# A gated cross-attention block on one core: filler matmuls ahead of three more waits at the start, two GpSimd subtractions cut in halves, and a new written order for every engine

## What is computed

```python
# stage 0: one wide head over the context, a gate, an RMS norm
memory_proj = einsum('bme,de->bmd', memory, W_mem)
scores = einsum('bnd,bmd->bnm', hidden_states, memory_proj) / sqrt(256)
memory_context = einsum('bnm,bmd->bnd', softmax(scores), memory_proj)
gate = sigmoid(einsum('bnf,df->bnd', concat([hidden_states, memory_context]), W_gate) + b_gate)
x = rmsnorm(hidden_states + gate * memory_context, norm_w)
# stage 1: 16 heads of 64, masked keys
q = layernorm(x, ln_q_g, ln_q_b) @ Wq * 64 ** -0.5
k, v = split(media @ Wkv)
sim = where(media_mask, q k^T, min_float)
x = x + tanh(attn_gate) * (softmax(sim) v @ Wo)
# stage 2: feed-forward of width 1024
h = gelu(layernorm(x, ln_ff_g, ln_ff_b) @ W1) @ W2
return x + tanh(ff_gate) * h
```

## Time and profile before

| | |
|---|---|
| time, median of 3 runs | 209.27 us (209.02 to 211.89) |
| time of the profiled execution | 210.25 us |
| its span (first to last instruction) | 208.4 us |
| PE busy | 202.4 us, 97% |
| DVE, ACT, POOL busy | 148.0, 130.5, 71.3 us |

### The profile page before, as it was taken

The page is one execution under the profiler, slowest core; times in us unless marked ns, Lnnn a source line. Parts: engine busy times, 40 slices in busy tenths (PEclk is TensorE's granted clock), DMA queues, the critical chain, the costliest instruction groups (busy, mean ns, idle before and its releaser), DMA issues.

```text
span 208.4 us, 4502 instructions
## 1 busy us (share of the span) xinstructions
PE 202.4 (97%) x1505; PEld 169.1 (81%) x1505; DVE 148.0 (71%) x529; ACT 130.5 (63%) x414; POOL 71.3 (34%) x71
## 2 busy tenths in 40 slices
PE   7999999999999999999999999999999999999993
PEld 3567868888689799787978988888886799988992
DVE  1779997779967698778698889997479673235310
ACT  4386757849766787665665838979996820168300
POOL 2010423853336244407140664685725006000000
PEclk9999999999999999999999999999999999999999
DMA  6995060050000000000000000015000001100001
GB/s 184 301 378 193 5 203 0 5 201 0 0 3 2 3 2 0 5 2 3 0 2 3 0 2 3 0 32 174 2 0 3 0 0 34 48 25 0 24 32 58
DMA packets 9297, 10.06 MB, mean 48 GB/s; under 512 B 1330, under 2 KB 8116, under 8 KB 9268
## 3 DMA queue, kind: packets, MB, share of 16 engines
q1 hardware_dynamic: 8468, 9.32, 13.4%
q10 hardware_dynamic: 800, 0.39, 0.6%
HBM read 8.66 MB, written 1.05 MB: 47 GB/s over the span
## 4 chain that ended last, share of the span: by engine, by line
PE 90%; DMA 4%; DVE 2%; SPq 2%; issue 0%
PE bank L513 57%; PE bank L1338 9%; PE bank L1310 8%; PE bank L1452 8%; DMA ctx_sb<-in_ctx_dram 4%; PE bank L1348 3%; PE bank L1293 2%; PE bank L1378 2%; SPq L560 2%; PE bank L1218 1%; PE bank L1231 1%; DVE wkv_lo L1069 1%; DVE x_sb L1171 0%; PE bank L1364 0%; DVE ctx_probsT_even L1014 0%
## 5 line engine op out<-in xcount | busy, mean ns | idle before, releaser
L630 POOL TENSOR_TENSOR probs<-expd,row_rcp 128x512 f32<-128x512 f32 x39 | 40.2, 1050 | 54.4 <-DVE row_rcp L1004 49.7
L760 ACT ACTIVATE expd<-expd,neg_max 128x128 f32<-128x128 f32 x128 | 49.6, 392 | 2.4 <-DVE neg_max L994 2.4
L994 DVE CUSTOM_DVE_ANT_0 expd<-bank,mask_bias 128x128 f32<-128x128 f32 x128 | 28.2, 286 | 2.2 <-PE bank L1310 2.1
L513 PE MATMUL bank<-xhT_pair,wq_pair 128*128 128x256 f32 x192 | 26.1, 289 | 0.0
L513 PE MATMUL bank<-wo_pair,oT_pair 128*128 128x256 f32 x192 | 26.0, 288 | 0.0
L513 PEld LDWEIGHTS bank<-xhT_pair,wq_pair 128*128 128x128 f32 x192 | 23.8, 191 | 2.0 <-issue 1.2
L760 ACT ACTIVATION_READ_ACCUMULATOR expd<-expd,neg_max 128x1 f32 x128 | 24.5, 191 | 0.0
L513 PEld LDWEIGHTS bank<-wo_pair,oT_pair 128*128 128x128 f32 x192 | 23.9, 190 | 0.5 <-issue 0.4
L513 PE MATMUL bank<-wq_pair,gelu_pair 128*128 128x256 f32 x192 | 23.6, 284 | 0.1
L513 PEld LDWEIGHTS bank<-wq_pair,gelu_pair 128*128 128x128 f32 x192 | 23.3, 192 | 0.5 <-DVE x_sb L1171 0.4
L1338 PE MATMUL bank<-ident,probs 128*128 128x128 f32 x160 | 21.1, 275 | 0.0
(11 more groups left out here) (163 smaller groups left out, 358.5 us busy)
## 6 DMA issues: line engine op xcount, KB each, us to landing
...
```

Of the source, the lines that this page charges most:

```text
L513: last = nc.tensor.matmul(bank_ap, lhs(a), rhs(c), start=start and n == 0, stop=stop and n == 2)
L630: nc.gpsimd.tensor_tensor(probs[:, r, :].rearrange("p (h k) -> p h k", h=hb), expd[:, r, :].rearrange("p (h k) -> p h k", h=hb), row_rcp[: ...
L760: last = nc.scalar.activation(here, here, ACT.Exp, bias=neg_max[:, r, h:h + 1], scale=-1.0, accum_out=row_sum[:, r, h:h + 1])
L994: last = nc.vector.tensor_tensor_reduce(expd[:, r, h * w:(h + 1) * w], SC[n % 2][:, h * w:(h + 1) * w], mask_bias[:, first:first + w], -1. ...
```

## The change

1. `DUMMIES` has five entries instead of two: 2, 1 and 2 identity matmuls stand ahead of `("ctxT", 0)`, `("tiles",)` and `("y", 0)`; the groups of 3 and 2 stay, the second now ahead of `("weights",)`.
2. On POOL the subtraction of `splitv` (1024 columns) becomes two of 512, and each of the two `splito` too; the semaphore rises with the second.
3. All four orders are new from the first stages to the last.

```diff
-DUMMIES = (3, 2)
+DUMMIES = (2, 1, 2, 3, 2)
 TENSOR_ORDER = (
-    ("xT", 0), ("ctxT", 0), ("y", 0), ("tiles",), ("ctxT", "hot"), ("scores", "ctx", 0, 0), ("look", "PE"),
-    ("branch", "PE"), ("dummy", 0), ("v", "hot", 0, 0), ("dummy", 1), ("v", "hot", 0, 1), ("ctxT", 1),
...
+    ("xT", 0), ("dummy", 0), ("ctxT", 0), ("dummy", 1), ("tiles",), ("dummy", 2), ("y", 0), ("look", "PE"),
+    ("branch", "PE"), ("ctxT", "hot"), ("scores", "ctx", 0, 0), ("dummy", 3), ("v", "hot", 0, 0), ("dummy", 4),
...
 POOL_ORDER = (
-    ("branch", "POOL"), ("norm", "ctx", 0, 0), ("splitv",), ("rms", 0), ("norm", "ctx", 1, 0), ("splito", 0),
+    ("norm", "ctx", 0, 0), ("branch", "POOL"), ("splitv",), ("rms", 0), ("norm", "ctx", 1, 0), ("splito", 0),
...
                         gp.wait_ge(pe["v"], 2)
-                        nc.gpsimd.tensor_tensor(wkv_lo[:, INNER:2 * INNER], wkv_sb[:, INNER:2 * INNER],
-                                                value_hi[:, :].bitcast(F32), ALU.subtract).then_inc(pool["kvlo"], 1)
+                        for half in (slice(0, BANK), slice(BANK, INNER)):
+                            of_kv = slice(INNER + half.start, INNER + half.stop)
+                            last = nc.gpsimd.tensor_tensor(wkv_lo[:, of_kv], wkv_sb[:, of_kv],
+                                                           value_hi[:, half].bitcast(F32), ALU.subtract)
+                        last.then_inc(pool["kvlo"], 1)
                     elif st[0] == "splito":
                         gp.wait_ge(act["wsplit"], path.split_no(st))
-                        nc.gpsimd.tensor_tensor(wo_pair[:, LO, cols_of(st)], stage[:, cols_of(st)],
-                                                wo_pair[:, HI, cols_of(st)].bitcast(F32), ALU.subtract
-                                                ).then_inc(pool["wsplit"], 1)
+                        for at in (st[1] * 1024, st[1] * 1024 + BANK):
+                            last = nc.gpsimd.tensor_tensor(wo_pair[:, LO, at:at + BANK], stage[:, at:at + BANK],
+                                                           wo_pair[:, HI, at:at + BANK].bitcast(F32), ALU.subtract)
+                        last.then_inc(pool["wsplit"], 1)
```

More of the change, by code:

```diff
@@ L33 @@
 WARM_UP = 8
-DUMMIES = (3, 2)
+DUMMIES = (2, 1, 2, 3, 2)
 TENSOR_ORDER = (
-    ("xT", 0), ("ctxT", 0), ("y", 0), ("tiles",), ("ctxT", "hot"), ("scores", "ctx", 0, 0), ("look", "PE"),
-    ("branch", "PE"), ("dummy", 0), ("v", "hot", 0, 0), ("dummy", 1), ("v", "hot", 0, 1), ("ctxT", 1),
[L47 to L65, removed]
[7 rows of a table removed]
-)
@@ new lines @@
+    ("xT", 0), ("dummy", 0), ("ctxT", 0), ("dummy", 1), ("tiles",), ("dummy", 2), ("y", 0), ("look", "PE"),
+    ("branch", "PE"), ("ctxT", "hot"), ("scores", "ctx", 0, 0), ("dummy", 3), ("v", "hot", 0, 0), ("dummy", 4),
+    ("weights",), ("v", "hot", 0, 1), ("spread", "ctx", 0, 0), ("xT", 1), ("gatemem",), ("u", 0), ("k", "hot", 0),
+    ("ctxT", 1), ("k", "hot", 1), ("gate", 0), ("k", "hot", 2), ("k", "hot", 3), ("y", 1), ("v", "hot", 1, 0),
+    ("k", "hot", 4), ("scores", "ctx", 1, 0), ("k", "hot", 5), ("k", "hot", 6), ("xhT", 0), ("k", "hot", 7),
@@ new lines @@
+    ("v", "hot", 1, 1), ("xT", 2), ("spread", "ctx", 1, 0), ("q", 0, 0), ("u", 1), ("scores", "head", 0, 0),
+    ("q", 0, 1), ("q", 0, 2), ("scores", "head", 0, 1), ("gate", 1), ("scores", "head", 0, 2), ("v", "hot", 2, 0),
+    ("q", 0, 3), ("spread", "head", 0, 0), ("ctxT", 2), ("scores", "head", 0, 3), ("av", 0, 0), ("y", 2),
+    ("spread", "head", 0, 1), ("v", "hot", 2, 1), ("scores", "ctx", 2, 0), ("wo", 0, 0), ("xhT", 1), ("av", 0, 1),
+    ("v", "hot", 3, 0), ("spread", "head", 0, 2), ("q", 1, 0), ("q", 1, 1), ("scores", "head", 1, 0), ("av", 0, 2),
@@ new lines @@
+    ("spread", "head", 0, 3), ("q", 1, 2), ("spread", "ctx", 2, 0), ("ctxT", 3), ("scores", "head", 1, 1),
+    ("xT", 3), ("u", 2), ("scores", "head", 1, 2), ("av", 0, 3), ("gate", 2), ("spread", "head", 1, 0), ("y", 3),
+    ("wo", 0, 1), ("q", 1, 3), ("wo", 0, 2), ("spread", "head", 1, 1), ("xhT", 2), ("av", 1, 0),
+    ("scores", "head", 1, 3), ("wo", 0, 3), ("q", 2, 0), ("scores", "ctx", 3, 0), ("q", 2, 2),
+    ("spread", "head", 1, 2), ("av", 1, 1), ("scores", "head", 2, 0), ("q", 2, 1), ("spread", "head", 1, 3),
@@ new lines @@
+    ("wo", 1, 0), ("spread", "ctx", 3, 0), ("scores", "head", 2, 1), ("av", 1, 2), ("u", 3), ("v", "hot", 3, 1),
+    ("scores", "head", 2, 2), ("gate", 3), ("spread", "head", 2, 0), ("q", 2, 3), ("wo", 1, 1), ("wo", 1, 2),
+    ("av", 1, 3), ("scores", "head", 2, 3), ("xhT", 3), ("av", 2, 0), ("wo", 1, 3), ("spread", "head", 2, 1),
+    ("q", 3, 0), ("q", 3, 1), ("scores", "head", 3, 0), ("av", 2, 1), ("wo", 2, 0), ("q", 3, 2),
+    ("spread", "head", 2, 2), ("q", 3, 3), ("scores", "head", 3, 1), ("av", 2, 2), ("spread", "head", 2, 3),
[5 rows of a table added]
@@ L142 @@
 POOL_ORDER = (
[L143 to L144 removed]
+    ("norm", "ctx", 0, 0), ("branch", "POOL"), ("splitv",), ("rms", 0), ("norm", "ctx", 1, 0), ("splito", 0),
+    ("xhat", 0), ("splito", 1), ("norm", "head", 0, 0), ("norm", "head", 0, 1), ("rms", 1), ("norm", "head", 0, 2),
     ("norm", "head", 0, 3), ("norm", "ctx", 2, 0), ("norm", "head", 1, 0), ("xhat", 1), ("norm", "head", 1, 1),
[L146 removed]
@@ L147 @@
-    ("ln2", 0), ("xhat", 2), ("rms", 3), ("norm", "head", 2, 1), ("norm", "head", 2, 2), ("xhat", 3), ("x2hat", 0),
-    ("norm", "head", 2, 3), ("ln2", 1), ("norm", "head", 3, 0), ("x2hat", 1), ("norm", "head", 3, 1),
+    ("rms", 2), ("xhat", 2), ("norm", "head", 1, 2), ("norm", "head", 1, 3), ("norm", "ctx", 3, 0),
+    ("norm", "head", 2, 0), ("rms", 3), ("ln2", 0), ("norm", "head", 2, 1), ("norm", "head", 2, 2), ("xhat", 3),
+    ("norm", "head", 2, 3), ("ln2", 1), ("x2hat", 0), ("norm", "head", 3, 0), ("x2hat", 1), ("norm", "head", 3, 1),
```

100 lines of the change are left out of this document (49 added, 51 removed), and 35 rows, old and new, of tables (SCALAR_ORDER, TENSOR_ORDER, VECTOR_ORDER).

## The result

The changed kernel takes 210.88 us (median of 23 runs, 209.91 to 214.26), the kernel before 209.74 us (median of 23 on the same chips, lowest 208.99). The ratio is 1.0050 with a 95% interval of 1.0033 to 1.0067: about 1.1 us slower, less than two per cent, near the forecast of 211.0. The ratio leaves out executions more than 1.5% above the fastest of their kernel: three of the changed kernel (213.33 to 214.26) and one of the kernel before (686.8, whose cause isn't known).

A forecast was written before the change was run, and what follows sets the result against it. The prediction took the kernel as a PE matmul stream behind a prologue that transfers dictate. +1.57 + 0.2 - 0.1 = +1.7 us on a median of 209.27 gave 211.0 us, own range 210.0 to 212.0, 8 in 10 range 209.4 to 213.2.

The forecast's parts named there:

- The wait and its place: Prologue: PE meets the W_gate wait behind the first value product and fillers, idling about 2.4 us until 13.8.
- Second value product, `spread`, batch 1's transposes, the hole: Work moved behind W_gate's landing, less the hole before the first key matmul: +1.57 us, first gate matmul near 21.45.
- To the first `q`, +0.2: First gate to first q product: waits of some 0.65 us against about 0.45 before; +0.2, between 0 and +1.0.
- Behind it, -0.1 with no new hole: Behind the first q: one fewer change between head and full matmuls, -0.1 us; no new holes, +1.5 the bound.
- Halves and fillers, 0: POOL's halved subtractions, between 2.04 and 2.41 us for two, and the new fillers inside the wait: 0 cost.
- The look, hidden: Prologue: PE stands about 0.8 us at the look at the flag, inside the W_gate wait, costing nothing.
- The landing: Prologue: SP's loads are untouched, so W_gate is taken to land where it did, at 13.8 us.
- Absorbed: Rival: DVE sets the pace from 20 to 34 us, so late PE catches up; 209.8 us, chance 0.17.
- Transfers land earlier: Rival: transfers land earlier in unprofiled runs; 210.4, or about 208.9 if 2.4 us sooner; chance 0.08 below 209.3.
- The clock falls in the wait: Rival: PE's idle 2.4 us at W_gate lowers the clock; 212.7 us, or 214.3 if twice as long; chance 0.12.
- signs that I had called wrong: W_gate transposes before 13, wait reached after 12, clock below 1 from 11 to 20, first q before 34.3, head idle tenths.

The follow-up runs named there:

- e1: The changed kernel once more, no edit; 211.05 us, ratio 1.0059 to the kernel before.
- e3: The changed kernel's lists up to the first gate, then the order of the kernel before, POOL's subtractions whole; 211.12 us, ratio 1.0060 to the kernel before.
- e6: The changed kernel without its three new filler groups; 210.81 us, ratio 1.0066 to the kernel before.
- the first profile: The profiled execution of the unedited kernel before, from which the prediction was made; 210.25 us.
- e7: The changed kernel with POOL's subtractions whole again, 1024 columns each; 211.29 us, ratio 1.0081 to the kernel before.
- f4: The changed kernel with W_gate loaded early, hotpair and splitk later on ACT (behind first value copy) and DVE (behind context 0's norm); 211.52 us, ratio 1.0061.
- e5: The changed kernel with SP's load of W_gate issued ahead of the other batches' context rows; 210.81 us, ratio 1.0062 to the kernel before.
- e4: The changed kernel with PE's second value product moved back ahead of the transposes of W_gate; 212.42 us, ratio 1.0116 to the kernel before.
- e2: The lists of the kernel before up to the first gate, then the changed order for the rest; 210.68 us, ratio 1.0047 to the kernel before.
- e8: The kernel before with batch 1's transposes of x moved ahead of the first key product on PE; 213.82 us, ratio 1.0187 to the kernel before.
- f1: The kernel before once more, no edit, on a chip with more scatter; 210.90 us, ratio 1.0028 to the same kernel.
- late transfer: The changed kernel's first profiled execution, unedited, in which batch 0's context rows landed late, at 8.26; 214.26 us.

## Why the prediction was right, and where its terms were off

**The wait and its place** were right: PE meets `W_gate` behind the first value product and fillers, released by its DMA, and all that used to fill that time comes behind. The landing to the gate is 7.67 us in e1, e3 and e6; the forecast's 21.45 behind 13.8 is 7.65.

**Second value product, `spread`, batch 1's transposes, the hole** (+0.86, +0.86, +0.32, -0.47): at the landing of the first profile, 13.76, the gate would come at 21.43 with 0.32 owed. That is +1.23 and +0.32, against +1.57.

**To the first `q`, +0.2**: measured, gate to `q` is 13.14 (20.87 to 34.01), with one value product, 0.70, not yet done, against 14.12 before: -0.28. The step that failed is the arrival at `xhat`. The mask's cast does stand where I put it, ahead of the first tanh, but hardly anybody waits: the tanh starts 1.99 behind the gate, not 2.45. I had the transposes of `xhat` wait to 31.5, 10.05 behind the gate of 21.45; they start 9.84 behind it. In e1, after ACT's rows, PE's:

```profile
21.05 1.92 ACT L720 ACTIVATE mask_bias<-mask_u 128x2048 bf16<-128x2048 uint8 x1
22.86 0.39 ACT L784 ACTIVATE th<-bank 128x256 f32<-128x256 f32 x1
```

```profile
30.27 0.40 PE L512 MATMUL bank<-hot_hi,wkv_lo 128*128 128x512 f32 x1
30.71 0.65 PE L1381 MATMUL bank<-ident,xhat 128*128 128x128 f32 x4
```

They start 0.44 behind their predecessor, a wait of 0.2. One thing that I had put at 0 goes the same way: the DVE instruction that took 1.07 beside POOL's subtraction takes 0.42 now that `splitv` is done before it. The halves don't do that, the new place does; that it makes the -0.28 is likely and not shown.

**Behind it, -0.1 with no new hole**: there is one new hole, in front of a product of probabilities and values at 134.5:

```profile
134.51 1.08 PE L1455 MATMUL bank<-probsT,v_sb 128*64 128x256 f32 x8 [0.39 <-DVE oT_pair L1106]
```

Behind the first `q` are 171.59 us against 170.37, of which 0.70 is the value product and 0.32 the owed transposes: +0.20, not -0.1. All that lies behind the gate together, the 0.32 owed among it, is 184.73 less 184.50, +0.23; the forecast had +0.32 + 0.2 - 0.1 = +0.42. The two terms were off by -0.5 and +0.3 and partly cancel.

**Halves and fillers, 0**: right within the intervals of e6 and e7. The halves' own duration, 2.51, lies 0.10 above the upper end of the 2.04 to 2.41 that I gave.

**The look, hidden**: right in e1, where the hot rows landed at 8.51 and PE took them at 8.56. In f4 they landed at 8.04 and PE took them at 8.90, in e5 at 7.26 and 8.00, in e4 at 7.80 and 8.97; in each 0.52 is a wait put down to issue. So with early rows the look is not free. The 1.02 of DVE from which I took its length wasn't the look: by its own row DVE waited there for PE's transposes.

**The landing** is the term of the sum that was mis-sized. Taken at the first profile's 13.76, the sum is +1.46 (1.23 + 0.23), against my +1.7. But the old order follows the hot rows and the new one follows `W_gate`, and the first profile had the two furthest apart, 6.23 us; with the load of `W_gate` in its usual place they are 5.65 apart in e2, 5.70 in e8 and 4.57 to 4.84 in all others. For f1's landings the new order would have its end at 13.30 + 7.67 + 184.73 = 205.70, against 205.49 measured for the old: +0.2. (f1's execution was itself a late one, 210.94 us against a median of 210.10 for its kernel on that chip.) The timed +1.1 lies between +0.2 and +1.5. Which distance the unprofiled runs had can't be seen, so how often each price is paid stays open. Nor is it shown that the landings are the same under both orders: all six profiled executions with the new start have them 4.68 to 4.84 apart, three of the five with the old start 5.65 to 6.23. These are too few to tell chance from an effect of the order. The forecast came within 0.2 of the result partly because too large a sum (+1.7) was set on a median of three runs that was low (209.27, later 209.74).

**The rivals.** *Absorbed*: no. Behind the gate the late PE gives back nothing of its own start: 184.80 in e3, and 184.74 or 184.75 in e4, e5 and e6 with the gate anywhere from 19.99 to 22.61. The 0.9 that the later order loses on the old start alone (e2) isn't won back by a late PE either. *Transfers land earlier*: they do, by 0.2 to 1.3, and more in e5; it made the loss smaller than my sum and not nil, in e5 because of the `spread`'s wait for POOL. *The clock falls in the wait*: not in this wait. It is 1.2 us long in e1, the granted clock is 1.00 through the stretch. Where PE idled for 2.82 us (late transfer) and 2.83 (e8) the granted clock fell to 0.50, the lower of the two levels, for 3.4 and 6.8 us. e7's wait of 2.06 was followed by a fall too, f1's of 1.70 was not. With a wait of 2.4, as I foresaw it, the chance would have been larger than 0.12. The Trainium skill (TensorE: Matmul & The Clock Gate, HAM oscillation) has waits for a DMA send the clock back. The first profile of the changed kernel and e7 agree (2.82 and 2.06 us, both for a DMA; e8's wait was for DVE); e1's wait of 1.2 and f1's of 1.70, for DMAs too, were followed by no fall.

Of the signs that I had called wrong, three appeared: PE reached the wait at 12.06, after 12; in e6 the transposes of `W_gate` began at 12.48, before 13; and the first `q` came at 34.01, before 34.3. A fourth, a clock below 1 behind 11, stands in the first profiled execution alone, to 11.57. They tell of landings, the third in part also of the -0.28. They were poor signs of a wrong mechanism, since they hang on one execution's transfers.
